# An attention-plus-MoE block on one core: where VectorE makes the causal-and-member mask of a head's widest step

## The reference, cut to what matters

```
q = (x @ wq) ...; k = (x @ wk) ...; v = (x @ wv) ...
logits = (x @ wr) ...                       # 4 nodes per head
tk_vals, tk_idx = top_k(logits, 2)
member = one_hot(tk_idx, 4).sum(-2) > 0
pos = cumsum(member) - member
for n in range(4):
    qr, kr = rotary(q, pos[n]), rotary(k, pos[n])
    scores = einsum(qr, kr) * SCALE
    scores = where(causal & member_of_column[n], scores, -1e9)
    outs.append(softmax(scores) @ v)
y = sum over the two chosen nodes of tk_w * outs
```

## Time and profile before

| what | value |
|---|---|
| median of 3 runs | 934.42 us (933.75 to 935.56) |
| profiled execution, its own time | 935.69 us |
| its span, first to last instruction | 934.0 us |
| granted TensorE clock, mean | 0.976 |
| PE / DVE / ACT / POOL busy | 828.7 / 792.5 / 732.8 / 605.6 us |
| one mask operation (line 1110), 128 of them | 454 to 475 ns, median 466 |

### The profile page before, as it was taken

One profiled execution on the slowest core, in us unless ns is written; L12 is line 12 of the kernel. 1 busy time (PEld: TensorE's weight loads), 2 busy tenths in 40 slices (PEclk: granted clock), 3 DMA queues, 4 the chain that ended last, 5 costly groups with the idle time before them and its releaser, 6 DMA issues.

```text
span 934.0 us, 21302 instructions
## 1 busy us (share of the span) xinstructions
PE 828.7 (89%) x6552; PEld 582.7 (62%) x6552; DVE 792.5 (85%) x1996; ACT 732.8 (78%) x2001; POOL 605.6 (65%) x951
## 2 busy tenths in 40 slices
PE   4458989999999999999999999999999999899893
PEld 4445656566656666666666666666666666565793
DVE  7859978998889889988998899879988887787795
ACT  7248888789888888888888888888898887865572
POOL 4556668776866676667666766676556666127393
PEclk9779999999999999999999999999999999999997
DMA  9001111111111121112111111111101110323553
GB/s 220 27 16 30 36 25 37 34 36 34 38 37 36 31 41 36 36 31 39 35 37 32 38 36 36 33 38 30 13 11 15 17 16 12 126 69 92 144 163 115
DMA packets 81039, 45.01 MB, mean 48 GB/s; under 512 B 35072, under 2 KB 79808, under 8 KB 80928
## 3 DMA queue, kind: packets, MB, share of 16 engines
q1 hardware_dynamic: 79712, 41.15, 19.9%
q0 software_dynamic: 1216, 2.51, 0.8%
HBM read 30.62 MB, written 12.43 MB: 46 GB/s over the span
## 4 chain that ended last, share of the span: by engine, by line
PE 49%; DVE 24%; ACT 11%; issue 10%; POOL 4%; DMA 1%; SPq 0%; DVEq 0%; ACTq 0%; POOLq 0%
PE psum L1539 17%; PE psum L1563 8%; PE psum L1392 7%; ACT probs L768 5%; PE psum L1552 5%; DVE pcs L1087 5%; DVE accs L1137 3%; POOL R L530 3%; PE psum L1524 3%; DVE negmax L1116 2%; PE psum L1588 2%; PE psum L1543 2%; DVE psum L1126 2%; ACT QK L745 1%; DVE probs L1205 1%
## 5 line engine op out<-in xcount | busy, mean ns | idle before, releaser
L1539 PE MATMUL psum<-QK 128*128 128x128 f32 (+3 forms) x1024 | 369.1, 452 | 5.6 <-DMA wrow<-words 4.4
L768 ACT ACTIVATE probs<-psum,negmax 128x128 f32<-128x128 f32 (+3 forms) x512 | 267.2, 530 | 70.3 <-DVE negmax L1126 49.8
L530 POOL TENSOR_TENSOR R<-pcs 128x512 f32<-128x512 f32 x128 | 176.3, 1399 | 54.4 <-DVE pcs L1087 54.4
L1539 PEld LDWEIGHTS psum<-QK 128*128 128x128 f32 x1024 | 158.9, 191 | 51.0 <-issue 46.3
L556 POOL TENSOR_TENSOR coef<-rden,wslot 128x2 f32<-128x2 f32 x256 | 53.2, 208 | 183.6 <-DVE rden L1132 183.6
L1137 DVE SCALAR_TENSOR_TENSOR accs<-probs,coef,accs 128x128 f32<-128x128 f32 (+3 forms) x256 | 166.6, 651 | 2.6 <-ACT accs L777 2.6
L777 ACT ACTIVATE accs<-probs,coef 128x128 f32<-128x128 f32 (+3 forms) x256 | 148.6, 581 | 17.6 <-POOL coef L556 17.3
L1087 DVE TENSOR_TENSOR pcs<-psum,arena 128x512 f32<-128x512 f32 x256 | 161.8, 673 | 0.0
L1552 PE MATMUL psum<-ident,accs 128*128 128x128 f32 x640 | 116.4, 280 | 39.0 <-DVE accs L1137 20.4
L1116 DVE TENSOR_REDUCE negmax<-psum 128x2 f32<-128x256 f32 (+1 forms) x128 | 70.4, 550 | 60.7 <-PE psum L1543 59.8
L745 ACT ACTIVATE QK<-psum 128x384 f32<-128x384 f32 x235 | 116.7, 497 | 1.3 <-PE psum L1526 1.2
(11 more groups left out here) (272 smaller groups left out, 1558.5 us busy)
## 6 DMA issues: line engine op xcount, KB each, us to landing
weight_halves<-whl SPq DMA_DIRECT2D x48, 128.0 KB, 2.2
arena<-weight_halves SPq DMA_DIRECT2D x22, 256.0 KB, 3.1
wrow<-words SPq DMA_DIRECT2D x64, 86.0 KB
arena<-weight_halves SPq DMA_DIRECT2D x7, 512.0 KB, 7.0
wrow<-words SPq DMA_DIRECT2D x64, 42.0 KB
wst<-in_L_ffn_w_up_dram SPq DMA_DIRECT2D x14, 128.0 KB, 2.4
wst<-in_L_ffn_w_gate_dram SPq DMA_DIRECT2D x14, 128.0 KB, 2.4
wst<-in_L_ffn_w_down_dram SPq DMA_DIRECT2D x14, 128.0 KB, 2.4
```

What stands on the lines that cost most here:

```text
L530: pool.tensor_tensor(R[u][:, :, :, 0:3:2, half * HALF:(half + 1) * HALF].rearrange("p t e j f -> p (t e) j f"), halves(pc, half), halves(p ...
L768: act.activation((expB if e else expA)[:, k % (4 if e else 3), 0:w], area, ACT.Exp, scale=1.0 if k % TB < 2 else -1.0, bias=negmax[k % 4][ ...
L1539: pe.matmul(o, QK[:, u, e, rows], QK[:, u, 2, 0:w], start=True, stop=False)
```

## The change

`place_outside` is called at another place of DVE's loop. Before, it was called for head n in step s = 3 of head n, in front of `row_max`. Now it is called for head n + 1 at the end of step s = 3 of head n, behind `row_max`, `weigh_b` and `inverse_sums`. The mask of head 0 is made in step 0, behind its `row_max`. The number of operations is the same. As the one tile `outside` is read by the row extremes of head n - 1, a wait for these (`negmax_done`) is added in front.

```diff
             def place_outside(n):
 
                 dve.wait_ge(S["codes_done"], 2)
+                if n:
+                    dve.wait_ge(S["negmax_done"], 2 * TB * n)
                 dve.wait_ge(S[f"mm_in{n % RING}"], 48 * (n // RING + 1))
...
-                if k < STEPS and s == TB - 1:
-                    place_outside(n)
                 if k < STEPS:
                     row_max(k)
...
                 if 1 <= k <= STEPS:
                     inverse_sums(k - 1)
+                if k == 0:
+                    place_outside(0)
+                elif s == TB - 1 and n + 1 < NH:
+                    place_outside(n + 1)
                 if k >= 1 and angle_tile(k - 1) is not None:
                     size_angles(angle_tile(k - 1))
```

## The result

The changed kernel takes 922.3 us (median of 4 runs, 920.22 to 923.56). The kernel before took 934.99 us in its 4 runs on the same chip. The ratio is 0.9856 with a 95% interval of 0.9823 to 0.9889; on the median of 934.42 us it makes 921.0 us. So the kernel is faster by 1.44%, some 13 us. The forecast was 9.1 us, and the low end of its range, 921.8 us, is 0.8 us above these 921.0. The direction and the place of the gain hold, and the forecast size is too small. In a second comparison on another chip the ratio was 0.9854 [0.9829, 0.9879].

The account below looks back on a forecast made before the run. DVE and PE set the chain in turn, with the mask operations a link in 12 pairs of heads. Gains of 7.2, 1.2 and 0.7 us sum to 9.1 us, giving a median of 925.3 us, range 921.8 to 931 us.

Parts of the forecast that it names:

- the place: Step s=3 of even heads with angles: without the mask pair, row extremes and ACT's exponentials start 0.78 us earlier.
- Rival 1: The pair stays in PE's path through the weighing behind it; result 934.4 us, give or take 1; chance 10%.
- the cover: Before s=0 of even heads DVE waits 1.25 us for PE; the moved pair hides there, leaving 0.47 us.
- what doesn't gain: Pairs starting at heads 4 or 6 mod 8: ACT's sines or POOL's coefficient come last, so 14 pairs gain nothing.
- Rival 3: Moved mask pairs hold POOL up by 0.45 us, 28 pairs lose 12.6 us; result 938 us; chance 6%.
- the collisions: DVE's shifted weighing of 128 columns meets POOL, 0.33 us; the 256-column weighing may come free; sum taken as nothing.
- Rival 2: DVE and POOL collide in each of 12 pairs, leaving 0.27 of 0.6 us; result 930.2 us; chance 12%.
- How much of it arrives: Odd head, s=1: DVE's 0.44 us of idle time plus 0.14 us before PE's flip, 0.6 us gained per pair.
- the 12 pairs: Pairs starting at even heads 8, 10, 16, 18, ..., 48, 50, with the mask pair in the chain; forecast gain 7.2 us.
- the first heads: Heads 0 to 3: the gain is the idle time before s=1 of heads 1, 2 and 3, 1.2 us.
- the highest gain: Upper bound: 0.78 us per pair and in head 60, 1.4 us early, 0.4 in head 62; 11.9 us, or 922.5 us.
- Heads 60 and 62: End of the attention: about 0.6 us gained in head 60 and 0.1 us in head 62, 0.7 us in all.

Follow-up runs that it names:

- Run 1: Changed kernel, but only even heads' masks made early, odd heads' masks left in front of their own row extremes; 922.16 us, ratio 0.9853 to the kernel before.
- run 3: Changed kernel with the mask pair done twice in even heads from 20 on, first into scratch; 928.58 us, ratio 0.9925 to the kernel before.
- run 4: Changed kernel with size_angles moved a step later, behind the s=3 extremes, in all heads with angles; 926.33 us, ratio 0.9886 to the kernel before.
- run 5: Run 1 with size_angles moved a step later in even heads alone; 918.55 us, ratio 0.9826 to the kernel before.
- Run 6: Changed kernel with one more mask-like DVE operation before the s=1 extremes of 12 odd heads; 926.27 us, ratio 0.9897 to the kernel before.
- run 7: Run 1 with the extra DVE operation of run 6 before the s=1 extremes; 922.75 us, ratio 0.9862 to the kernel before.

## Why the prediction was right or wrong

*Right: the place.* The first row extreme starts where size_angles ends (351.26 behind 350.94), ACT's idle time in front of the exponentials went from 0.91 to 0.12 us, and PE's 1.44 us to 0.66 us, now with ACT's copy named as releaser. Rival 1 is refuted by one row pair: the weighing of 256 columns is 0.36 us later in the table above, and PE is 0.78 us earlier. The name in the earlier trace rows was indeed wrong. Run 1 shows that this half of the move is the whole gain.

*Right: the cover.* The idle time before s = 0 of even heads went from 1.25 to 0.48 us (forecast 0.47), and run 3 shows that it is cover for that much and no more.

*Right: what doesn't gain.* The pairs of heads 4 and 6 mod 8 are the same from head 12 on. Rival 3 would have shown there, and doesn't: it is refuted. POOL's line 535 takes 1.04 us in head 24 as in the earlier trace rows, with the mask pair no longer beside it, and line 542, beside which the pair now falls, takes 0.62 us in both kernels.

*Right in kind: the collisions.* The weighing of 128 columns did fall beside POOL's line 538 (0.34 to 0.71 us), and that of 256 came free of POOL's line 542 (0.88 to 0.47 us). The exchange is not quite zero: the two weighings together are 0.04 us shorter. Rival 2 is refuted. The Trainium skill ("SBUF — State Buffer", section "Who interferes with whom") says that a VectorE instruction with two SBUF inputs contends with a GpSimd instruction that reads SBUF; the weighing's longer times beside POOL agree. The same section's warning about `tensor_scalar` has no counterpart for the mask pair in these rows, but it has one for size_angles, also a `tensor_scalar`. Runs 4 and 5 show it in head 24:

```profile
354.58 0.62 POOL L542 TENSOR_TENSOR ktoks<-kwork,cgap 128x256 f32<-128x256 f32 x1
354.64 0.84 DVE L1074 TENSOR_SCALAR arena<-arena 128x512 uint32<-128x512 uint32 x1
```

```profile
349.80 0.86 POOL L538 TENSOR_TENSOR kwork<-R 128x256 f32<-128x256 f32 x1
350.07 0.87 DVE L1074 TENSOR_SCALAR arena<-arena 128x512 uint32<-128x512 uint32 x1
```

It begins beside an operation of POOL and ends 0.28 us behind that operation's end in both (355.48 behind 355.20, 350.94 behind 350.66). In its old place it began first and kept its 0.40 us, and POOL's coefficient beside it took 0.29 to 0.30 us instead of 0.20. So this collision exists here too, but it falls into runs 4 and 5 and not into the change.

*Wrong: the step "How much of it arrives".* It took DVE's idle time before s = 1, 0.44 us, as a cap on what passes through DVE, added the 0.14 us to spare between copy and flip, and got 0.6 us per pair. Measured: 0.79 us. In the prediction's own terms, the sum should have been:

- 0.44 us of idle time,
- 0.07 us by which that idle time is counted too short (the prediction priced the mask pair from start to start, 0.78 and not 0.86 us, and this wait not),
- 0.05 us by which DVE's queue behind the pair is shorter, most of it from the collisions (taken as nothing),
- 0.08 us between DVE's extremes and ACT's exponentials (not looked at: ACT was itself late, so DVE wasn't what it waited for),
- 0.06 us by which ACT's copy ends sooner behind the start of its exponentials (not to be seen in the trace of before),
- 0.09 of the 0.14 us behind the copy, since 0.79 us is all that PE can get.

That is 0.79 us. The last three terms are one stretch of spare time, 0.28 us before the change, of which 0.23 us are used and 0.05 us left. Run 6 measured what is left, 0.05 us (0.33 us of delay gives 0.28 at the flip), and run 7 the whole stretch, 0.27 us, in a kernel whose DVE isn't late. How the 0.23 us divide between the hand-overs holds for this pair and most of the others, not for all. Nor does the gain follow the idle time from pair to pair: that is 0.11 us in head 11, 0.80 in head 17 and 0.58 in head 33 of the kernel before, and these pairs gained 0.72, 0.77 and 0.78 us. The term for the 12 pairs was therefore 2.3 us too small, 9.5 for 7.2, and this alone is more than half of the miss.

*Wrong: the same cap in the first heads.* There I took DVE's idle time before s = 1 of heads 1, 2 and 3 as the gain: 1.2 us. It was 1.93 us up to head 4. The idle time is gone there as forecast. But from one s = 0 to the next, head 0 lost 0.44 us, head 1 gave 0.36, head 2 gave 0.87 and head 3 gave 1.14 us, and in runs 3 and 6, with the same code, head 0 gave 0.32 us instead, which makes 2.7 us up to head 4. By which way the surplus comes wasn't tested; that it is the spare time of the point above is only argued.

*Wrong: head 4.* The prediction gave its pair nothing, because heads 28 and its like gain nothing. But in head 4 the mask pair stood in the chain, and the prediction itself counted it there. It gave 0.46 us.

*Wrong: the highest gain.* The prediction put it at 11.9 us, and the attention gained 13.2. The first heads alone passed their 1.4 us by 1.0; the 12 pairs and what lies between them gave 9.8 us for 9.4. So the low end of the range was missed by the first heads above all.

*Heads 60 and 62:* 1.03 for 0.7 us. Head 60 with 0.52 us is near the forecast of 0.6, and the end gave 0.5 us for 0.1.

*Outside the attention.* From the last extreme to the end of the span it is 122.9 us before and 121.9 us after. What follows the attention is the same code in both. The changed kernel had a granted TensorE clock of 1.00 in the window from 820 to 870 us and the kernel before 0.97. Over all profiles here this tail takes 121.9 to 125.6 us, the two longest with a clock of 0.93 in that window (runs 4 and 6), so some 3.7 us by which these two lie above the changed kernel aren't in the attention. Nothing of the change works there, so I count none of it as a gain of the change.

## What to carry to other kernels

Idle time of an engine in the middle of a chain isn't a cap on what passes through it. The cap is that idle time and every spare moment behind it, up to what was taken off: ask at each hand-over whether the next engine started because the work was ready, or because it was free itself. A start that comes 0.19 us behind its input where 0.11 us is the usual distance has 0.08 us to spare. Count from start to start where operations overlap at their ends: idle time read as 0.44 us was 0.51 us here. And an operation that is taken off one chain lengthens the queue of the next: run 4 lost its 0.31 us so, and run 5 kept them by leaving the odd pair where it had been.

## What the runs showed of the hardware that I hadn't expected

DVE and POOL hold each other up in both orders, and which operation began first decides which is longer. Wherever runs 4 and 5 start size_angles beside POOL's line 538 or 542 (28 and 14 places), it ends 0.28 to 0.29 us behind that operation and lasts 0.44 to 0.88 us, against 0.40 us where it begins first. The extra operation of runs 6 and 7, on 16-bit elements, ends 0.14 to 0.16 us behind the one beside it in all 24 places, with 0.40 to 0.84 us. The mask pair, on 16-bit elements too, keeps its 0.84 to 0.87 us wherever it stands.

A copy or exponentials of ACT of one shape have more than one recorded duration. In head 25 the copy of 128x384 took 0.55 us before and in run 1, and 0.49 us in the changed kernel and in runs 6 and 7; the exponentials of 128x256 in front of it 0.52 and 0.47 us. From start to next start both take nearly the same, 0.37 and 0.44 to 0.47 us, so it is the recorded end that moves. The longer one appears where the exponentials follow ACT's weighing at once; what makes it longer wasn't tested.

The granted clock between 0 and 66 us, a mean over the stretch in which 1.00 would be the upper level throughout, was 0.82 before, 0.83 in the changed kernel and 0.91 in run 1, with the same instructions there. And between 820 and 870 us it was 0.93 in three kernels (runs 3, 4 and 6) whose code after the attention is the same as in the others:

```profile
820.00:870.00 50.00, 44.63 (x445) 31.80 (x443) 36.88 (x75) 28.26 (x51) 23.64 (x26) 0.93 0.31 89
```

This is run 4, with the busy time of PE, PEld, DVE, ACT and POOL and, behind them, the granted clock. The changed kernel:

```profile
820.00:870.00 50.00, 42.98 (x485) 30.76 (x483) 40.01 (x77) 28.99 (x52) 24.49 (x27) 1.00 0.35 97
```

What makes the difference stayed open. It is why a total time of one run can mislead by 2 to 3 us here, and the time of a pair of heads past the first ones much less: where nothing of a run touches it, it repeats within 0.03 us.
